# Attention scores from float32r row halves, two units at a time, in a fused attention and expert layer

## What is computed

```python
qkv = (x @ Wqkv).reshape(b, l, 3, H, DH)            # b=8, l=512, H=16, DH=16
q = q * cos + rotate_half(q) * sin
k = k * cos + rotate_half(k) * sin
scores = jnp.einsum('bqhd,bkhd->bhqk', q, k) * DH ** (-0.5)
attn = jax.nn.softmax(scores, axis=-1)
out = jnp.einsum('bhqk,bkhd->bqhd', attn, v).reshape(b, l, d)
```

## Time and profile before

| | |
|---|---|
| median of 3 runs | 1292.8 us (1289.08 to 1293.45) |
| the profiled execution, span | 1291.3 us |
| attention, about | 0 to 565 us, of it full periods from about 50 to 535 us |
| norm, routing, experts, combine | the rest |
| PE, DVE, ACT, POOL busy in 200 to 300 us | 100.0, 82.5, 92.3, 27.3 us |

### The profile page before, as it was taken

One profiled execution on the slowest core, in us unless ns is written; L12 is line 12 of the kernel. 1 busy time (PEld: TensorE's weight loads), 2 busy tenths in 40 slices (PEclk: granted clock), 3 DMA queues, 4 the chain that ended last, 5 costly groups with the idle time before them and its releaser, 6 DMA issues. The chain is left out here.

```text
span 1291.3 us, 29542 instructions
## 1 busy us (share of the span) xinstructions
PE 1224.3 (95%) x9440; PEld 934.5 (72%) x9440; DVE 976.6 (76%) x1925; ACT 996.4 (77%) x2043; POOL 583.9 (45%) x590
## 2 busy tenths in 40 slices
PE   4899999999999999979899969999999999999997
PEld 3444444444444444337899969999999999999897
DVE  6888887888788888728676648777777777777596
ACT  6699998999899999846654437777777777777687
POOL 6332322232223220005467745666666666666763
PEclk8899999999999999988899979999999999999999
DMA  9300000010000000433022246777777777776363
GB/s 298 117 19 19 18 19 20 2 35 3 19 2 19 2 18 3 144 104 117 18 91 100 87 158 197 260 251 253 246 238 238 235 249 253 253 239 217 101 218 119
DMA packets 125414, 161.28 MB, mean 125 GB/s; under 512 B 17088, under 2 KB 108224, under 8 KB 125312
## 3 DMA queue, kind: packets, MB, share of 16 engines
q1 hardware_dynamic: 118496, 141.25, 33.7%
q0 software_dynamic: 6816, 18.75, 4.1%
HBM read 122.06 MB, written 37.52 MB: 124 GB/s over the span
## 5 line engine op out<-in xcount | busy, mean ns | idle before, releaser
L546 DVE TENSOR_REDUCE att_mx<-att_psA 128x1 f32<-128x512 f32 x512 | 337.8, 683 | 75.5 <-PE att_psA L331 74.9
L461 ACT ACTIVATE att_prob<-att_psB 128x512 f32<-128x512 f32 x512 | 299.7, 600 | 54.0 <-PE att_psB L341 41.0
L341 PE MATMUL att_psB<-att_qk 128*128 128x512 bf16 x512 | 197.6, 388 | 12.8 <-issue 5.6
L1648 ACT ACTIVATE exp_psU<-exp_psU,ew_b 128x256 f32<-128x256 f32 x312 | 126.6, 447 | 103.7 <-PE exp_psU L1605 103.7
L331 PE MATMUL att_psA<-att_qk 96*128 96x512 bf16 x512 | 196.9, 386 | 3.0 <-DVE att_mx L546 3.0
L1699 DVE CAST exp_hh<-exp_psU 128x512 fp32r<-128x512 f32 x156 | 107.9, 692 | 101.9 <-ACT exp_psU L1648 101.9
L1588 PE MATMUL exp_psD<-exp_w2h,exp_hh 128*128 128x256 f32 x624 | 175.8, 282 | 0.0
L1603 PE MATMUL exp_psU<-exp_xh,exp_w1h 128*128 128x256 f32 x624 | 173.7, 278 | 1.4 <-DVE exp_xl L1690 1.4
L1605 PE MATMUL exp_psU<-exp_xh,exp_w1l 128*128 128x256 f32 x624 | 173.4, 278 | 0.0
L1604 PE MATMUL exp_psU<-exp_xl,exp_w1h 128*128 128x256 f32 x624 | 173.3, 278 | 0.0
L1589 PE MATMUL exp_psD<-exp_w2l,exp_hh 128*128 128x256 f32 x624 | 172.4, 276 | 0.0
(11 more groups left out here) (215 smaller groups left out, 3244.9 us busy)
## 6 DMA issues: line engine op xcount, KB each, us to landing
ew_w<-ew SPq DMA_DIRECT2D x40, 1024.0 KB, 6.1
exp_w<-ew SPq DMA_DIRECT2D x38, 1024.0 KB, 5.8
slots_x<-pre_acc SPq DMA_DIRECT2D x13, 780.0 KB, 10.8
pre_spare<-slots_x SPq DMA_DIRECT2D x39, 260.0 KB, 4.1
out_g<-rows_y SPq DMA_DIRECT2D x32, 256.0 KB, 4.1
ew_b<-eb SPq DMA_DIRECT2D x39, 128.0 KB
pre_spare<-xT SPq DMA_DIRECT2D x8, 512.0 KB, 4.5
attn_rows<-att_ob SPq DMA_DIRECT2D x8, 512.0 KB, 2.8
```

Of the source, the lines that this page charges most:

```text
L341: pe.matmul(psB[B_BANK[n % U]][:, :], r[:, 1, kt * P:(kt + 1) * P], r[:, 0, :], start=True, stop=True).then_inc(s_bmm, 1)
L461: act.activation(prob[:, n % PR, :], psB[B_BANK[n % U]][:, :], ACT.Exp, scale=SCALE).then_inc(s_exp, 1)
L546: dve.reduce_max(mx[:, g % 2, n % U:n % U + 1], psA[A_BANK[n % U]][:, :], AX_X).then_inc(s_max, 1)
```

## The change

Queries and keys are cut into two float32r pieces instead of three bfloat16 pieces; three products remain (48 contraction rows instead of 96), and the maximum takes two rows. `qk` now holds two heads at once, one in partitions 0 to 63 and one in 64 to 127. The units of a group are dealt out so that a column works on one half while the row beside it works on the other, and PE's code takes two units together: column, row, column, row, and only then the other work. PE turns two heads in one float32r matmul against the identity (`turn_pair`, 128 stationary columns, four for the queries and four for the keys of two heads), and ACT copies 128x512 (`copy_pair`). POOL writes the first pieces twice itself and makes the second ones; `piece_1`, `piece_2`, `spread`, `split_max` and the start-up rows of ones are gone. The maxima are turned as they are and split in `copy_max`, which now has two dependent instructions; four DMAs place them. The order of `psX` becomes projection, maximum, output, value, and `ob`, the output's staging buffer, is single.

```diff
-    TERMS = 6
+    TERMS = 3
     KR = TERMS * DH
+    PIECES = 2
+    KC = KR + PIECES
+    HALF = P // 2
...
-    T_LEAD = A_LEAD + 5
-    PIECES = 3
-
-    PROJECT_QK, ROPE, COPY_OUT, TURN_OUT, NORM_OUT = (0, 1), (1, 2, 3), 3, 5, (5, 6)
-    PROJECT_V, COPY_V, SPLIT_MAX, TURN_MAX, COPY_MAX = 13, 13, 8, 10, 9
-    PIECE_1, PIECE_2, SPREAD, SPLIT_X = 6, 10, 0, 12
+    T_LEAD = A_LEAD + 8
+
+    PROJECT_QK, TURN_MAX, TURN_OUT, PROJECT_V = (0, 4), 8, 10, 12
+    ROPE, COPY_MAX, NORM_OUT = (5, 6, 7), 9, (11, 12)
+    COPY_OUT, COPY_V, SPLIT_X = 4, 14, 12
...
-        stack = a.sb("stack", [P, 2, NT, 2, H, KR], BF16)
-        qk = a.sb("qk", [P, RING, 2, G, L], BF16)
+        stack = a.sb("stack", [P, 2, ROWS], F32R)
+        qk = a.sb("qk", [P, RING, 2, PAIRS, L], F32R)
...
-        ob = a.sb("ob", [P, 2, NT, D], F32)
+        ob = a.sb("ob", [P, NT, D], F32)
...
                 for k in range(PIECES):
-                    sp.dma_start(qk[96 + k:97 + k, g % RING, 0, :, :].rearrange("o j (t c) -> o (j t) c", c=P),
-                                 mrow[k * U:(k + 1) * U, g % 2, :]).then_inc(s_mld[g % 2], 16)
+                    for j in range(2):
+                        row = half_of(j) + KR + k
+                        sp.dma_start(qk[row:row + 1, g % RING, 0, :, :].bitcast(F32).rearrange("o j (t c) -> o (j t) c", c=P),
+                                     mrow[j * U // 2:(j + 1) * U // 2, g % 2, k, :].bitcast(F32)).then_inc(s_mld[g % 2], 16)
...
+            def split(tile, it):
+                b, t = tile // NT, tile % NT
+                if tile >= FILL:
+                    wait(pool, it, s_qrd, tile + 1, 1)
...
+                    pool.tensor_tensor(rr[:, tile % 2, :], rc[:, :], rs[:, :], ALU.add).then_inc(s_rr, 1)
+                    for i in range(2):
+                        write_high(b, t, i, lambda out, *sides: pool.tensor_tensor(out, *sides, ALU.add), rc, rs).then_inc(s_hi, 1)
+                for i in range(2):
+                    wait(pool, it, s_hi, 2 * tile + i + 1, 2)
+                    pool.tensor_tensor(low(b, t, i), heads_of_part(rr[:, tile % 2, :], i), stacked(b, t, i)[:, :, 0:DH].bitcast(F32),
+                                       ALU.subtract).then_inc(s_lo, 1)
...
-                r = qk[0:KR, g % RING, :, h % G]
+                r = qk[half_of(j):half_of(j) + KR, g % RING, :, pair]
...
-                r = qk[:, g % RING, :, j]
+                r = qk[half_of(j):half_of(j) + KC, g % RING, :, j // 2]
...
-                    m = pe.transpose(psT[0:KR, half, t * P:(t + 1) * P], stack[:, b % 2, t, half, h % H, :], ident[:, :])
...
+                    m = pe.matmul(psT[:, t * P:(t + 1) * P], stack[:, b % 2, at:at + P], ident[:, :], start=True, stop=True)
...
-                wait(pe, it, s_msp, g + 1, 1)
-                pe.matmul(psX[0:PIECES * U, 0:P], mstk[:, :, :].rearrange("p m u -> p (m u)"), ident[:, :], start=True, stop=True).then_inc(s_mtr, 1)
+                wait(pe, it, s_max, U * (g + 1), U)
+                pe.transpose(psX[:, 0:P], mx[:, g % 2, :], identf[:, :]).then_inc(s_mtr, 1)
...
-                for u in range(U):
+                for u in range(0, U, 2):
+                    for n in (p * U + u, p * U + u + 1):
+                        if valid(n, NG * U):
+                            score_cols(n, it)
+                        if valid(n + A_LEAD, NG * U):
+                            score_rows(n + A_LEAD, it)
...
-                act.activation(qk[0:KR, g % RING, :, h % G, :], psT[0:KR, :, :], ACT.Copy).then_inc(s_tev, 1)
...
+                act.activation(qk[:, g % RING, i, pair, :], psT[:, :], ACT.Copy).then_inc(s_tev, 1)
...
-                dve.tensor_copy(mrow[:, g % 2, :], psX[0:PIECES * U, 0:P]).then_inc(s_mev, 1)
+                link(dve.tensor_scalar(mrow[:, g % 2, 0, :], psX[0:U, 0:P], -1.0, None, ALU.mult))
+                linked(it)
+                dve.scalar_tensor_tensor(mrow[:, g % 2, 1, :], psX[0:U, 0:P], -1.0, mrow[:, g % 2, 0, :].bitcast(F32),
+                                         ALU.mult, ALU.subtract).then_inc(s_mev, 1)
```

More of the change, by code:

```diff
@@ L152, in attention @@
         s_onrm = a.sem("o_normed")
-        s_ost = [a.sem(f"o_stored{i}") for i in range(2)]
-        s_tmm = a.sem("head_turned")
-        s_tev = a.sem("head_ready")
-        s_msp = a.sem("max_split")
+        s_ost = a.sem("o_stored")
+        s_tmm = a.sem("pair_turned")
+        s_tev = a.sem("pair_ready")
         s_mtr = a.sem("max_turned")
@@ L162, in attention @@
         s_rr = a.sem("qk_turned")
-        s_p1 = a.sem("piece_1")
-        s_r1 = a.sem("rest_1")
-        s_p2 = a.sem("piece_2")
-        s_p3 = a.sem("piece_3_q")
-        s_qsp = a.sem("qk_split")
-        s_stk = a.sem("stacked")
+        s_hi = a.sem("qk_hi")
+        s_lo = a.sem("qk_lo")
         s_vmm = a.sem("v_projected")
@@ L203, in heads_of, with stacked, half_of, high @@
             return t[:, :].rearrange("p (h d) -> p h d", d=DH)
-        def terms(stack, b, t):
-            return stack[:, b % 2, t].rearrange("p i h (m d) -> p (i h) m d", d=DH)
+        def stacked(b, t, i):
+            at = (t * 2 + i) * H * HALF
+            return stack[:, b % 2, at:at + H * HALF].rearrange("p (h m) -> p h m", m=HALF)
+        def half_of(j):
+            return HALF * (j % 2)
+        HI = ((0, 16), (0, 32))
+        LO = (32, 16)
+        def high(b, t, i):
+            first, second = HI[i]
+            return stacked(b, t, i)[:, :, first:second + DH].rearrange("p h (m d) -> p h m d", d=DH)[:, :, ::second // DH, :]
+        def low(b, t, i):
+            return stacked(b, t, i)[:, :, LO[i]:LO[i] + DH]
+        def heads_of_part(v, i):
+            return v[:, i * D:(i + 1) * D].rearrange("p (h d) -> p h d", d=DH)
+        def write_high(b, t, i, op, *sources):
+            return op(high(b, t, i), *(heads_of_part(v, i).unsqueeze(2).to_broadcast([P, H, 2, DH]) for v in sources))
         block = pr.block
@@ L274, in _ @@
         def _(pool):
+            pads = [stack[:, b, 0:ROWS].rearrange("p (t i h m) -> p t i h m", i=2, h=H, m=HALF) for b in range(2)]
             for k, step in enumerate((
[L277 to L279 removed]
                 lambda: pool.memset(identf[:, :], 0.0),
@@ L524, in period @@
                         copy_v(p + V_LEAD, it)
-                    if u == SPREAD and valid(p + QK_LEAD - 1, NT * B):
-                        spread(p + QK_LEAD - 1, it)
             groups(act, period)
@@ L531, in _ @@
         def _(dve):
-            LINKS = 4
+            LINKS = 2
             done = [0]
@@ L633, in _, with period @@
             dve.wait_ge(s_tab, 32)
-            def fill(tile):
+            def period(p, it):
+                tile = p + QK_LEAD
                 if tile < FILL:
@@ L639, in fill @@
                         rope(tile, k, None)
-                if tile > 0:
-                    piece_2(tile - 1, None)
-                if tile < FILL:
                     add_turned(tile)
-                    piece_1(tile, None)
-            def period(p, it):
-                if p + QK_LEAD <= FILL:
-                    fill(p + QK_LEAD)
-                    if p + QK_LEAD < FILL:
-                        return
+                    return
                 for u in range(U):
@@ L654, in period @@
                         row_max(n + A_LEAD, it)
-                    if u in ROPE and valid(p + QK_LEAD, NT * B):
-                        rope(p + QK_LEAD, ROPE.index(u), it)
-                    if u == PIECE_1 and valid(p + QK_LEAD, NT * B):
-                        piece_1(p + QK_LEAD, it)
-                    if u == PIECE_2 and valid(p + QK_LEAD, NT * B):
-                        piece_2(p + QK_LEAD, it)
+                    if u in ROPE and valid(tile, NT * B):
+                        rope(tile, ROPE.index(u), it)
+                    if u == COPY_MAX and valid(p + 1, NG):
+                        copy_max(p + 1, it)
                     if u in NORM_OUT and valid(p - 1, NG):
                         norm_out(p - 1, NORM_OUT.index(u), it)
-                    if u == SPLIT_MAX and valid(p + 1, NG):
-                        for k in range(4):
-                            split_max(p + 1, k, it)
-                    if u == COPY_MAX and valid(p + 1, NG):
-                        copy_max(p + 1, it)
             def after_loop():
```

209 lines of the change are left out of this document (82 added, 127 removed).

## The result

The changed kernel takes **1334.1 us** (1332.6 to 1335.6, four runs), the kernel before 1293.0 (1289.1 to 1293.5, four runs). The ratio is 1.0327, its 95% interval 1.0308 to 1.0346: 3.3% slower, 46 us above the forecast of 1288 and above its range.

The account below looks back on a forecast made before the run. PE's stream was taken to set attention's time. From 1291.3 us, 9 gained in the periods, 6 gained at the start and 10 lost in SP's queue gave 1286.3, plus 1.5 from profiled execution to median: 1288 us, range 1248 to 1322.

Parts of the forecast that it names:

- the queue of SP: Maxima DMAs stand behind a store waiting for `norm_out`: 1.5 us (0 to 2) in each of 7 periods, 10 us lost.
- the start: Before the first turn, a chain shorter by one POOL and three ACT steps: 6 us (3 to 8) gained.
- the rival without overlap: Scores: the two halves don't overlap, a block is 0.43 us longer, period 18.1, time 1360 us; chance 0.05.
- the 0.28 a pair: Scores: by the skill's 3.07 for four row tiles, a pair takes 0.28 instead of 0.22, some 1 us a period more.
- the rival of slow turns: Turned heads: float32r matmuls of 128 columns make four passes, a step 0.47 us longer, period 16.6, 1316 us; chance 0.12.
- The wait before the value projection: At u12, PE stands 0.5 us until `norm_out`, behind that row's maximum on DVE, ends at 13.3.
- The 0.9 before the turned output: At u10, PE stands 0.9 us after its block of scores, until DVE ends `copy_max` at 10.1.
- The price of a block: Four scores in overlapping halves: 0.19 us going in plus 2 x 0.22, 0.63; 8 blocks take 5.0 instead of 7.0.
- the gain of 9 us: Attention's period falls from 15.99 to 15.7 us, 0.3 less, over 30 periods.
- loads of the two halves in line: Scores: the second load waits for the first, a block grows by 0.1 us, period 16.2, time 1303 us; chance 0.09.
- The opposite rival: Blocks and turns: loads hide, a block pays only 0.06 us going in, period 14.7, time 1258 us; chance 0.33.
- The rival of the clock: Attention: PE, idle a tenth of the time, stays at 1.2 GHz for a tenth; some 45 us, 1330 us; chance 0.05.

Follow-up runs that it names:

- the first experiment: The changed kernel with one edit: SP places a group's maxima before it stores a finished sequence; 1304.5 us, 1.0127 times the kernel before.
- the series on one half: The changed kernel plus 48 extra matmuls on one row half in its last period, results unread; its time says nothing, the clock fell 5.5 us in.

## Why the prediction was wrong

The miss is 46 us: about 10 in the ordinary periods, 17 in the queue of SP, 17 in the start, 1 behind attention.

**What held.** PE stayed the bound, and what DVE and ACT gave up was worth nothing. Column and row overlap (same hundredth; in a long row of pairs 0.23), so the rival without overlap is out, and so is the 0.28 a pair that the prediction named beside its sum. Turns take 0.11, and the rival of slow turns is out. The wait before the value projection is 0.47 (0.5). The 0.9 before the turned output is 0.2 there and 0.4 at the second row of u8, which the walk through the period had passed over; the turned output still starts 10.3 into the period (10.1), and from u8 to u12 it takes 4.4 (forecast 1.4 + 2.2 + 0.9 = 4.5). u12 itself takes 2.55 (2.5).

**The price of a block failed.** The step read "0.19 + 2 x 0.22 = 0.63", with the load's 0.13 ahead of the first pair and the second pair hidden. The second pair is 0.335 instead. From `add_pv` to the next block it is 0.99 (305.27 to 306.26), where the forecast had 0.88 + 0.19 = 1.07; from a block's start to `add_pv` it is 0.67 (304.60 to 305.27), where it had 0.44 + 0.09 = 0.53. So the load put ahead of the first pair hardly shows, and more than it comes later: the steps of u2, u6 and u14 take 1.66 (forecast 1.60), u0 and u4 2.14 and 2.02 (1.96). Together that is 0.42 a period, 16.1 instead of 15.7, and the gain of 9 us became a loss of about 2. The nearest named rival was "loads of the two halves in line", with 16.2 a period. Its size was right and its mechanism wrong: in a row of pairs nothing waits, only the second pair behind a change of shape does. The opposite rival, that loads hide and a period takes 14.7, had a chance of 0.33 and is far off; the earlier trace rows had spoken against it.

**The queue of SP was mis-sized.** Mechanism and place were right: seven times PE waits for the maxima behind the store. But the forecast took 1.5 each, for the wait alone, and put what the clock does behind it at nothing. Against the first experiment the seven cost 3.5, 1.3, 2.0, 7.1 (with the 19th), 4.9, 1.9 and 6.6, together 27.3 or 3.9 a store. The two behind which the clock held cost 2.0 and 1.9: that is the wait, near the 1.5 of the forecast, and a little longer because the fourth DMA starts 2.6 us after the store and not 2.2 (the four stand 0.7 apart, not 0.59). By the same price seven waits are 14 us, and the other 13 go with the spells at 1.2 GHz.

**The start failed in sign.** Forecast was "6 us (3 to 8)" gained by a shorter chain. The chain did get shorter, by about as much: the first turned heads stand at 24.51 instead of 31.23, the first rows at 29.07 instead of 33.69. But the first turned maxima came 1.6 later and not earlier, and the two periods behind them were 9.8 longer, at 1.2 GHz until 84 us. The rival of the clock had named this effect, with a tenth of attention at half clock (here 61 us at the start and 51 later up to 572 us, nearly a fifth; before 31 in all), and was given 0.05 for "waits here are under 1 us at a time". That reason failed twice. The forecast had itself put waits of 1.5 us behind SP's queue. And PE can lose its clock without any wait, as the series on one half shows. At the start, where only rows are there to run and no columns (their maxima don't exist yet), the change has stretches like this one:

```profile
30.84 2.37 PE L349 MATMUL att_psA<-att_qk 48*128 48x512 f32 x4
```

Four scores in 2.4 us, one at a time. That is the worst of them: from 35 us on the first two rows of a step start together (35.57), and the third and fourth follow alone, 0.6 and 1.6 later. From 60 to 84 us all 32 scores of the trace start in pairs, and the clock is still 1.2 GHz. That such stretches, and then the pairs, keep the clock down at the start is likely but not shown by a run of its own; shown is that full-array work put there ends the spell about 50 us earlier.

**The clock and the busy share.** "TensorE: Matmul & The Clock Gate" of the Trainium skill, Part 1, says that the gate follows how busy PE has been and that activity releases it. With the profile's busy share taken for that activity, 60 to 80 us (19.7 of 20 busy) would be at 2.4 GHz, and the first periods near 16; the trace has 0.50 there and 21.5. A busy share of 99% in the profile did not go with 2.4 GHz here, and the measurement decides.

## What to carry to other kernels

Splitting the array pays going in, going out, and at the second float32r matmul behind either change: 0.42 to 0.45 us a block between full-array float32r work, whether it holds one pair or four. A pair saves 0.23, so a block of two pairs only breaks even; use few and long blocks. Before a DMA that PE waits for, nothing may stand on its queue that waits for a later product; moving two lines there was worth 27 us, twice what the waits alone cost, because a gap of PE of 2 us was followed by half clock five times of seven. And read the granted clock of the start and behind each stall before calling a kernel's cost understood: a like gap cost 1 us beyond itself in the full-array mix and nearly 3 in the half-array one.

## What the runs showed of the hardware

- Two matmuls on row halves start 2 to 5 ns apart (24 in the longest series), and pairs follow each other in 0.227 us over a long series, where one half alone takes 0.227: all of the overlap is had.
- A change of shape costs about 0.1 going in and about 0.1 going out at 2.4 GHz. The second float32r matmul or pair behind it, full-array or half, comes after 0.335 to 0.34 instead of 0.23, the second bfloat16 pair after 0.223.
- A float32r matmul of 128 columns takes 0.112, as much as a float32 transpose, and its load of 184 to 190 ns is twice that of bfloat16 (94).
- PE fell to 1.2 GHz at a busy share of 100%, on one row half alone, and was granted 0.50 for 40 us at the start at 90 to 99%. Two halves in turn, or 96 rows, held 2.4 GHz; two halves in turn, begun at 1.2 GHz, stayed there for 9.7 us.
- PE's loop edge costs 4.5 to 5 us in both kernels (periods of 20.8 and 20.6 among 16.0). Before, PE stands 2.9 and 2.8 us there for nothing that the profile shows, and 3.4 us at 1.2 GHz follow each time.
